# Softmax row sums taken by ones-products on TensorE, and casts, copies and normalising moved from VectorE to ScalarE

## The chip, the cores and the metric

The kernel runs on one core of one Trainium2 chip. The metric is the device time of one execution in microseconds (us); lower is better. Before the change it is 1401.03 us, the median of three runs (1400.17 to 1402.62).

## The reference, cut to what matters

Sixteen images of 256 x 256 go through an edge filter, 77 embedded text tokens are appended to each (333 rows of 256), and then come an attention layer over five windows of 128 rows and a mixture of eight experts:

```python
h = clip(sum(abs(conv2x2(x))), 0, 1)                 # (16, 256, 256)
h = concatenate([h, weight[x_txt]], axis=1)          # (16, 333, 256)
# attention, 16 heads of 16, windows of 128 rows with stride 64 (and the last 128 rows)
z = layernorm(h); q, k, v = z @ Wq + bq, z @ Wk + bk, z @ Wv + bv
scores = q_win @ k_win.T / sqrt(16) + pos_bias       # 128 x 128 for each head and window
out_win = softmax(scores) @ v_win
merged = scatter_add(out_win) / counts               # rows in two windows are averaged
h = h + merged @ Wo + bo
# experts: softmax gate, top 2 of 8, silu(x @ w1) * (x @ w3) @ w2, weighted and added
h = h + moe(layernorm(h))
```

## The kernel before, in words

All is written out by hand for five engines that run side by side and meet in semaphores. There are two stages. The first takes the images one after the other through the attention layer, the router and a scatter of the rows into regions by expert. The second takes 91 tiles of 128 rows through the expert products; the change does not touch its code.

**The first stage.** A loop `run_steps` calls `step(b, par)` for each image b on every engine, and inside it a loop over k = 0 to 19. One k, called a step here, stands for one group: a window (5 of them, `NW`) times four heads (`GH`), so 5 x 4 = 20 groups (`G`) for an image. The groups go through a pipeline, the same on every engine:

- TensorE at step k: scores of group k into `s_bank` (L1026, four bf16 products), transposes of the probabilities of group k-3 into `t_bank` (L1040, four), products with V of group k-4 into `o_bank` (L1063, four products of 32 columns of weights, one for each strip of 32 output rows; they show as eight records in the trace). On every fourth group of a window it also transposes a tile `weight` (L1072, two products).
- VectorE at step k: adds the bias to the scores of group k and takes the row minimum into `neg_max` (L757, a custom instruction and the reading of its accumulator, four of each).
- ScalarE at step k: exp of group k-1 with the row sum (L622, four ACTIVATEs, each followed by an ACTIVATION_READ_ACCUMULATOR), then the copy of the transposed probabilities of group k-2 to `probsT` (L636, three groups of four; the fourth is copied by VectorE in L772).

**The row sums before.** The row sums land as `row_sum` with the query rows on the partitions, while the outputs in `o_bank` have the head's columns on the partitions. So once for each window VectorE inverts 16 sums for each row (L768), spreads them over 256 columns as `weight` (L776), TensorE transposes that (L1072), ScalarE copies the transposed tile to `weightT` (L642), and VectorE multiplies it with the outputs into `head_out` (L784). GpSimd adds `head_out` to `ctxT` (L520).

**What else hangs on the steps.** Each step also carries work of neighbouring images at fixed k. On TensorE: transposes of the normalised rows `xn` (k = 0, L1082), the router's counting products (k = 2, L1089 and L1093), the Q and K projections (k = 2 to 5, L1104), the output projection (k = 6 and 7, L1004), the V projection (k = 10 and 11, L1011), transposes of the second layernorm's `rows` (k = 16, L1134), the gate product (k = 18, L1142). ScalarE moves `xT` (k = 0, L648), `qk` (k = 2 to 5, L660) and `x2T` (k = 16, L667) out of PSUM. VectorE does both layernorms' statistics and normalising (L714), the casts of `qk` into bf16 parts (L733, L738), V's bias (L745), absolute values of the filter (L851), and the router. GpSimd does the filter's differences, the splitting of `qk` into three bf16 parts (L502, L507), the inverse root, and the scatters.

**The stacks.** Q and K of an image enter the scores as bf16 parts stacked on 96 partitions. They go there by way of DRAM: SyncE's queue writes each part with two transfers (L366, `qk_parts`), and reads it back with six transfers for Q and six for K (L372, `stacks`). Before, it issues five of the six pairs of writes, then waits for all of Q's parts and reads them, then writes the last pair, stores the image's rows, waits for all of K's parts, and reads K. The scores of the next image wait for all twelve reads (`stack_in`).

## Time and profile before

| | |
|---|---|
| median of 3 runs | 1401.03 us |
| the profiled execution | 1394.69 us, its span 1392.9 us, the rest lies around the span |
| TensorE busy | 1189.1 us (85% of the span) |
| VectorE busy | 920.9 us (66%) |
| ScalarE busy | 782.9 us (56%) |
| GpSimd busy | 611.8 us (44%) |
| granted TensorE clock, mean | 0.919 |

The shares are averages over the two stages, which differ: read them apart. Times below are microseconds from the span's start. A start-to-start distance of two neighbouring rows of one engine says what an instruction takes of the engine's time; its own length is longer, since neighbours overlap.

### The profile page before, as it was taken

The page shows a single profiled execution, that of the slowest core. Times are in us where ns is not written, and L with a number is a line of the kernel's source. Part 1 is how long each engine was busy: PE and PEld are TensorE (multiplying, and loading weights), DVE is VectorE, ACT ScalarE, POOL GpSimd, SP SyncE. Part 2 cuts the span into 40 slices and gives each one's busy share as a digit, 9 for nine tenths or more (in the row PEclk, how much of TensorE's full clock was granted, in tenths as well). Part 3 has the DMA queues.
Part 4 walks back from the last instruction along what each step waited for, and adds up shares of the span by engine and source line. Part 5 has one row for each costly group of instructions (what it writes and reads, how often), then busy time and mean ns, then how long its engine had stood idle before and what let it go on. Part 6 is the DMA issues. An engine that isn't in the chain of part 4 may idle for free.

```text
span 1392.9 us, 35049 instructions
## 1 busy us (share of the span) xinstructions
PE 1189.1 (85%) x10190; PEld 951.8 (68%) x10191; DVE 920.9 (66%) x4211; ACT 782.9 (56%) x3176; POOL 611.8 (44%) x900
## 2 busy tenths in 40 slices
PE   2386888988988998888889872999999999999996
PEld 1254656655655665555556551999999999999995
DVE  4485989888888889898997864344444444444442
ACT  0196998989899998899899980211111111111110
POOL 5333466565646655665665334122322232232232
PEclk9698899889898988999998985899999999999998
DMA  3694563465357446634643507232233323323222
GB/s 110 133 234 100 109 132 89 95 131 113 88 103 142 92 92 116 128 89 94 133 107 71 96 24 234 36 50 46 49 47 48 49 45 49 48 46 48 46 49 31
DMA packets 98402, 123.36 MB, mean 89 GB/s; under 512 B 15544, under 2 KB 87416, under 8 KB 95192
## 3 DMA queue, kind: packets, MB, share of 16 engines
q1 hardware_dynamic: 75880, 89.96, 30.6%
q0 software_dynamic: 18576, 24.47, 10.9%
q10 hardware_dynamic: 3808, 7.34, 1.8%
q8 instruction: 57, 0.93, 0.3%
q14 instruction: 81, 0.66, 0.2%
HBM read 69.35 MB, written 46.07 MB: 83 GB/s over the span
## 4 chain that ended last, share of the span: by engine, by line
PE 47%; POOL 16%; issue 14%; DMA 12%; ACT 4%; SPq 3%; DVE 3%; POOLq 0%; DVEq 0%; ACTq 0%
PE s_bank L1168 12%; PE t_bank L1168 12%; PE o_bank L1183 11%; DMA qk_parts<-parts_flat 5%; POOL expert_slots L493 4%; DMA expert_slots<-rows,slot_i 4%; DMA stacks<-qk_parts 3%; PE m_bank L1104 3%; ACT probs L622 3%; PE t_bank L1040 2%; SPq L372 2%; POOL rest L502 2%; PE o_bank L1063 2%; POOL parts_flat L507 2%; PE m_bank L1157 1%
## 5 line engine op out<-in xcount | busy, mean ns | idle before, releaser
L622 ACT ACTIVATE probs<-probs,neg_max 128x128 f32<-128x128 f32 x1280 | 497.4, 401 | 21.6 <-DVE neg_max L757 21.0
L757 DVE CUSTOM_DVE_ANT_0 probs<-s_bank,nbias 128x128 f32<-128x128 f32 x1280 | 293.0, 284 | 38.4 <-PE s_bank L1026 36.9
L622 ACT ACTIVATION_READ_ACCUMULATOR probs<-probs,neg_max 128x1 f32 x1280 | 257.4, 201 | 0.0
L1040 PE MATMUL t_bank<-ident,probs 128*128 128x128 f32 x1280 | 221.0, 300 | 28.7 <-ACT probs L622 26.7
L681 ACT ACTIVATE v_all<-s_bank 128x512 f32<-128x512 f32 x91 | 54.4, 598 | 286.9 <-PE s_bank L1168 286.9
L1026 PE MATMUL s_bank<-stacks 96*128 96x128 bf16 x1280 | 136.5, 233 | 68.8 <-DMA stacks<-qk_parts 46.9
L1026 PEld LDWEIGHTS s_bank<-stacks 96*128 96x128 bf16 x1280 | 93.4, 105 | 132.4 <-DMA stacks<-qk_parts 50.7
L1040 PEld LDWEIGHTS t_bank<-ident,probs 128*128 128x128 f32 x1280 | 150.1, 153 | 45.7 <-ACT probs L622 41.7
L636 ACT ACTIVATE probsT<-t_bank 128x512 f32<-128x512 f32 x240 | 141.9, 591 | 57.5 <-PE t_bank L1040 56.7
L1183 PE MATMUL o_bank<-stacks,v_all 128*128 x728 | 172.6, 380 | 0.7 <-issue 0.5
L597 POOL DMA_INDIRECT out_dram<-wq_sb,nbias x46 | 75.7, 1645 | 198.5 <-DVE wq_sb L967 185.3
L1063 PE MATMUL o_bank<-probsT,v_all 128*32 128x128 f32 x2560 | 146.0, 303 | 16.9 <-ACT probsT L636 9.7
L597 POOL DMA_INDIRECT out_dram<-wk_sb,nbias x45 | 73.3, 1629 | 172.8 <-DVE wk_sb L967 170.0
L973 DVE TENSOR_TENSOR v_all<-v_all,t_bank 128x512 f32<-128x512 f32 x91 | 62.6, 688 | 127.1 <-PE t_bank L1168 127.1
L1183 PEld LDWEIGHTS o_bank<-stacks,v_all 128*128 128x128 f32 x728 | 131.3, 190 | 16.0 <-issue 1.8
L675 ACT ACTIVATE v_all<-m_bank 128x256 f32<-128x256 f32 x91 | 35.0, 384 | 143.3 <-PE m_bank L1157 143.3
L493 POOL DMA_INDIRECT expert_slots<-rows,slot_i x96 | 100.0, 1042 | 29.3 <-issue 21.7
L1063 PEld LDWEIGHTS o_bank<-probsT,v_all 128*32 128x32 f32 x2560 | 52.9, 112 | 79.0 <-issue 50.0
L757 DVE DVE_READ_ACCUMULATOR2_ANT neg_max<- 128x1 f32 x1280 | 103.8, 81 | 0.1
L1168 PEld LDWEIGHTS s_bank<-v_all,probs 128*128 128x128 f32 x736 | 91.0, 195 | 3.2 <-ACT v_all L675 0.9
L1168 PE MATMUL s_bank<-v_all,probs 128*128 128x128 f32 x736 | 91.4, 278 | 0.5 <-ACT v_all L675 0.5
L1168 PE MATMUL t_bank<-v_all,probs 128*128 128x128 f32 x736 | 90.7, 277 | 0.0
(158 smaller groups left out, 2079.4 us busy)
## 6 DMA issues: line engine op xcount, KB each, us to landing
stacks<-qk_parts SPq DMA_DIRECT2D x192, 166.5 KB, 5.6
qk_parts<-parts_flat SPq DMA_DIRECT2D x192, 83.2 KB
nbias<-expert_slots SPq DMA_DIRECT2D x91, 129.0 KB, 2.0
w_sb<-in_L_ffn_w_dram ACTq DMA_DIRECT2D x14, 512.0 KB, 5.2
v_all<-v_all SPq DMA_DIRECT2D x64, 96.0 KB, 6.4
x_here<-in_x_dram SPq DMA_DIRECT2D x16, 256.0 KB, 5.7
out_dram<-h_res SPq DMA_DIRECT2D x16, 256.0 KB
stacks<-in_L_ffn_w_dram SPq DMA_DIRECT2D x8, 512.0 KB, 8.5
```

The source lines that it names most:

```text
L493: pool.indirect_dma_start(slots_dram[:, :], bass.IndirectOffsetOnAxis(slot_i[0:n, kk, j:j + 1], 0), rows[0:n, kk, j, :], None).then_inc(sc ...
L597: pool.indirect_dma_start(out[:, :], bass.IndirectOffsetOnAxis(g_rows[r][:, D + 1:D + 2].bitcast(I32), 0), y_sb[r], None, compute_op=ALU.a ...
L622: ins = act.activation(seg, seg, ACT.Exp, bias=neg_max[:, r, i:i + 1], scale=-1.0, accum_out=row_sum[:, (par + v) % 2, h:h + 1])
L636: act.activation(probsT[:, k % 2, :], t_bank[:, k % 2, :], ACT.Copy).then_inc(pT_by_act, 1)
L681: act.activation(hidT[r % 2], s_bank[:, r % 2, :], ACT.Silu).then_inc(silu_ready, 1)
L757: ins = dve.tensor_tensor_reduce(probs[:, r, i * WIN:(i + 1) * WIN], s_bank[:, k % 2, i * WIN:(i + 1) * WIN], nbias[:, h, :], 1.0, BIG, AL ...
L973: dve.tensor_tensor(hidT[r % 2], hidT[r % 2], t_bank[:, r % 2, :], ALU.mult).then_inc(hid_ready, 1)
L1026: mm = pe.matmul(s_bank[:, k % 2, i * WIN:(i + 1) * WIN], q_stack[par][0:KROWS, h, lo:lo + WIN], k_stack[par][0:KROWS, h, lo:lo + WIN], st ...
L1040: mm = pe.transpose(t_bank[:, (k - 3) % 2, i * WIN:(i + 1) * WIN], probs[:, r, i * WIN:(i + 1) * WIN], ident[:, :])
L1063: mm = pe.matmul(o_bank[32 * i:32 * i + 32, vp, (g // 2) * WIN:(g // 2 + 1) * WIN], v_win[bp][:, w, c0:c0 + 2 * HD], probsT[:, (k - 4) % 2 ...
L1168: mm = pe.matmul(bank[:, par, n * P:(n + 1) * P], up_w[par][:, m, a, n * P:(n + 1) * P], gxT[par][:, a * P:(a + 1) * P], start=(a == 0), s ...
L1183: mm = pe.matmul(o_bank[:, r % 2, 0:D], hidT[r % 2][:, a * P:(a + 1) * P], w2_sb[:, bass.ds(e, 1), a, :].rearrange("p o n -> p (o n)"), st ...
```

## The change

- The row sums are no longer taken by exp. After the four products with V of a group, TensorE makes four more of the same form with a constant tile `head_of` of ones and zeros in the place of V. The sums then land in `o_bank` in the layout of the outputs, each repeated over the 16 columns of its head.
- VectorE inverts these, 128 columns at a time, twice a window, straight from PSUM into `weightT`, and multiplies. The tiles `row_sum`, `inv_sum`, `weight`, the transposes of `weight` and ScalarE's copy of them are gone.
- ScalarE copies all four groups of a window to `probsT`. It also takes over from VectorE: the high bf16 part (a second ACTIVATE out of PSUM beside that to `qk`), the middle part, the moving of V, the absolute values, and both normalisings, as ACTIVATEs with a scale and a bias for each row (the bias, minus mean times inverse root, is two instructions more on GpSimd).
- V's bias is folded into the output's bias once, with a product at the start.
- Several pieces stand at another k: ScalarE's moves of `xT` (0 to 1), `qk` (2-5 to 3-6), V (12, 13), `x2T` (16 to 17), the second normalising (VectorE's 14 to ScalarE's 15), the output projection (6, 7 to 7, 8), GpSimd's adding of a window (two steps later). The router's products go to `m_bank`.
- SyncE's queue reads each part back as soon as that part is written, with a semaphore for each part.

The core of the diff (names and constants, the first stage's other moves of k, and the counts of semaphores are left out):

```diff
 SyncE
-                    write_part(0, 0, part1_ready)
-                    write_part(1, 0, part1_ready)
-                    write_part(0, 1, part2_ready)
-                    write_part(0, 2, part3_ready)
-                    write_part(1, 1, part2_ready)
+                    write_part(0, 0, part1_ready, b1 * 4 + 2)
+                    write_part(1, 0, part1_ready, b1 * 4 + 4)
                     if b >= 1:
                         sp.wait_ge(scores_done, (b1 - 1) * G)
-                    load_stack(0, q_stack[par1], Q_SLOTS)
-                    write_part(1, 2, part3_ready)
+                    load_stack(0, 0, q_stack[par1], Q_SLOTS)
+                    write_part(0, 1, part2_ready, b1 * 2 + 1)
+                    load_stack(1, 0, k_stack[par1], K_SLOTS)
+                    write_part(0, 2, part3_ready, b1 * 2 + 1)
+                    load_stack(0, 1, q_stack[par1], Q_SLOTS)
+                    write_part(1, 1, part2_ready, b1 * 2 + 2)
+                    load_stack(0, 2, q_stack[par1], Q_SLOTS)
+                    write_part(1, 2, part3_ready, b1 * 2 + 2)
+                    load_stack(1, 1, k_stack[par1], K_SLOTS)
                     if tail:
                         store_h2()
-                    load_stack(1, k_stack[par1], K_SLOTS)
+                    load_stack(1, 2, k_stack[par1], K_SLOTS)
...
 ScalarE
+                def normalise(src, rstd, shift, dst, done):
+                    for j in range(NT):
+                        act.activation(dst(j), src[:, j, :], ACT.Identity, bias=shift[:, j:j + 1],
+                                       scale=rstd[:, j:j + 1]).then_inc(done, 1)
...
-                            ins = act.activation(seg, seg, ACT.Exp, bias=neg_max[:, r, i:i + 1], scale=-1.0,
-                                                 accum_out=row_sum[:, (par + v) % 2, h:h + 1])
+                            ins = act.activation(seg, seg, ACT.Exp, bias=neg_max[:, r, i:i + 1], scale=-1.0)
                         ins.then_inc(exp_ready, 1)
...
-                    if proj and k in (2, 3, 4, 5):
+                    if proj and k in (3, 4, 5, 6):
...
+                        for dst, done in ((qk[:, 2 * n + c, :], qk_ready), (parts[:, 2 * n + c, 0, :], part1_ready)):
+                            act.activation(dst, m_bank[:, c, 0:S], ACT.Identity,
+                                           bias=(bq_col if n == 0 else bk_col)[:, c:c + 1],
+                                           scale=(-SCALE if n == 0 else 1.0)).then_inc(done, 1)
+                    if proj and k == 7:
+                        part_middle(0)
+                    if proj and k == 9:
+                        part_middle(1)
...
+                    if tail and k == 15:
+                        act.wait_ge(rstd2_ready, b0 + 1)
...
+                        normalise(h_res[1 - par], rstd2, shift2, lambda j: rows[:, 0, j, 0:D], rows0_ready)
-                    if tail and k == 16:
+                    if tail and k == 17:
                         act.wait_ge(x2T_done, b0 + 1)
...
 VectorE
-                        dve.reciprocal(inv_sum[:, vp, :], row_sum[:, vp, :]).then_inc(inv_ready, 1)
-                        dve.tensor_copy(probsT[:, k % 2, :], t_bank[:, k % 2, :]).then_inc(pT_by_dve, 1)
-                        dve.tensor_copy(weight[:, vp, :, :], inv_sum[:, vp, :].unsqueeze(2).to_broadcast([P, H, HD]))\
-                            .then_inc(weight_ready, 1)
+                    v, c = ((k - 8) // NG, 0) if k % NG == 0 else ((k - 10) // NG, 1)
+                    if k % 2 == 0 and ((att and v >= 0) or (tail and v < 0)):
...
+                        dve.reciprocal(weightT[:, c * WIN:(c + 1) * WIN],
+                                       o_bank[:, vp, (C + c) * WIN:(C + c + 1) * WIN]).then_inc(inv_ready, 1)
+                        if c == 1:
...
+                            dve.tensor_tensor(head_out[:, vp, :], o_bank[:, vp, 0:C * WIN], weightT[:, :], ALU.mult)\
+                                .then_inc(head_ready, 1)
...
 TensorE
+                        for i in range(GH):
+                            mm = pe.matmul(o_bank[32 * i:32 * i + 32, vp, (C + g // 2) * WIN:(C + g // 2 + 1) * WIN],
+                                           head_of[:, (g % 2) * HD:(g % 2) * HD + 2 * HD],
+                                           probsT[:, (k - 4) % 2, i * WIN:(i + 1) * WIN],
+                                           start=False, stop=(g % 2 == 1), skip_group_check=True)
                         mm.then_inc(pv_done, 1)
-                        if g == 3:
-                            pe.wait_ge(weight_ready, b * NW + m // NG + 1)
-                            for c in range(C):
-                                mm = pe.transpose(o_bank[:, vp, (C + c) * WIN:(C + c + 1) * WIN], ...)
...
-                            pe.wait_ge(qk_ready, b1 * 4 + c + 1)
+                            pe.wait_ge(part1_ready, b1 * 4 + c + 1)
```

**TensorE, step k = 4.** Before, the K projection stands behind transposes and products whose results ScalarE moved at k = 2:

```order
L1026 MATMUL s_bank<-stacks 128x128 [waits max_ready]
L1026 MATMUL s_bank<-stacks 128x128 x3
L1040 MATMUL t_bank<-ident,probs 128x128 [waits pT_by_dve,exp_ready]
L1040 MATMUL t_bank<-ident,probs 128x128 x3
L1063 MATMUL o_bank<-probsT,v_all 32x128 [waits prefix_read,v_shift_in,head_ready,v_ready,pT_by_act]
L1063 MATMUL o_bank<-probsT,v_all 32x128 x3
L1104 MATMUL m_bank<-xT,wk_sb 128x333 [waits qk_ready]
L1104 MATMUL m_bank<-xT,wk_sb 128x333
```

Now, at the same place (the lines of the changed kernel are numbered anew; L1053 are the products with ones):

```order
L1018 MATMUL s_bank<-stacks 128x128 [waits max_ready]
L1018 MATMUL s_bank<-stacks 128x128 x3
L1029 MATMUL t_bank<-ident,probs 128x128 [waits pT_ready,exp_ready]
L1029 MATMUL t_bank<-ident,probs 128x128 x3
L1047 MATMUL o_bank<-probsT,v_all 32x128 [waits v_shift_in,head_ready,v_ready,pT_ready]
L1047 MATMUL o_bank<-probsT,v_all 32x128 x3
L1053 MATMUL o_bank<-probsT,head_of 32x128 x4
L1096 MATMUL m_bank<-xT,wk_sb 128x333 [waits part1_ready]
L1096 MATMUL m_bank<-xT,wk_sb 128x333
```

Four products came in, and the projection waits for the second of the two moves of ScalarE instead of the only one.

**ScalarE, steps k = 2 and 3.** Before, the first move of Q stands in k = 2, in front of the exp and the copy of k = 3:

```order
L622 ACTIVATE probs,row_sum<-probs,neg_max 128x128 [waits max_ready]
L622 ACTIVATE probs,row_sum<-probs,neg_max 128x128 x3
L636 ACTIVATE probsT<-t_bank 128x512 [waits pv_done,pT_done]
L660 ACTIVATE qk<-m_bank,bq_col 128x333 [waits rest_ready,qk_done]
L622 ACTIVATE probs,row_sum<-probs,neg_max 128x128 [waits max_ready]
L622 ACTIVATE probs,row_sum<-probs,neg_max 128x128 x3
L636 ACTIVATE probsT<-t_bank 128x512 [waits pv_done,pT_done]
```

Now k = 2 carries the absolute values (`diag`, `anti`), and the first move of Q, to `qk` and to `parts_flat`, stands behind the copy of k = 3:

```order
L655 ACTIVATE probs<-probs,neg_max 128x128 [waits max_ready]
L655 ACTIVATE probs<-probs,neg_max 128x128 x3
L667 ACTIVATE probsT<-t_bank 128x512 [waits pv_done,pT_done]
L677 ACTIVATE score_e<-below_best 128x24 [waits payload_ready,below_ready]
L681 ACTIVATE diag<-diag 128x512 [waits diffs_ready]
L681 ACTIVATE anti<-anti 128x512
L655 ACTIVATE probs<-probs,neg_max 128x128 [waits max_ready]
L655 ACTIVATE probs<-probs,neg_max 128x128 x3
L667 ACTIVATE probsT<-t_bank 128x512 [waits pv_done,pT_done]
L691 ACTIVATE qk<-m_bank,bq_col 128x333 [waits parts_out0_0,rest_ready,qk_done]
L691 ACTIVATE parts_flat<-m_bank,bq_col 128x333
```

The move went behind one more wait for TensorE's transposes (`pT_done`), and became two.

**SyncE's queue, the parts of one image.** Before, from the second pair of writes for Q on to the reading of K:

```order
L366 DMA qk_parts<-parts_flat 8x16x333 [waits part2_ready]
L366 DMA qk_parts<-parts_flat 8x16x333
L372 DMA stacks<-qk_parts 16x5328 [waits parts_out0,scores_done]
L372 DMA stacks<-qk_parts 16x5328 x5
L366 DMA qk_parts<-parts_flat 8x16x333 [waits part3_ready]
L366 DMA qk_parts<-parts_flat 8x16x333
L357 DMA out_dram<-h_res 128x2x256 [waits h2_ready]
L358 DMA out_dram<-h_res 77x256
L372 DMA stacks<-qk_parts 16x5328 [waits parts_out1]
L372 DMA stacks<-qk_parts 16x5328 x5
```

Now, in the middle of an image:

```order
L375 DMA stacks<-qk_parts 16x5328 [waits parts_out0_0,scores_done]
L375 DMA stacks<-qk_parts 16x5328 x2
L368 DMA qk_parts<-parts_flat 8x16x333 [waits part2_ready]
L368 DMA qk_parts<-parts_flat 8x16x333
L375 DMA stacks<-qk_parts 16x5328 [waits parts_out1_0]
L375 DMA stacks<-qk_parts 16x5328 x2
L368 DMA qk_parts<-parts_flat 8x16x333 [waits part3_ready]
L368 DMA qk_parts<-parts_flat 8x16x333
L375 DMA stacks<-qk_parts 16x5328 [waits parts_out0_1]
L375 DMA stacks<-qk_parts 16x5328
L368 DMA qk_parts<-parts_flat 8x16x333 [waits part2_ready]
L368 DMA qk_parts<-parts_flat 8x16x333
```

Reads that stood behind all writes of Q now stand between the writes, each with a wait for its own part.

## Rows read from the trace of the kernel before

**Rows 1.** Busy us by stretch: PE, PEld, DVE, ACT, POOL; clock, DMA share, GB/s.
```profile
0.00:63.00 63.00, 11.85 (x34) 7.83 (x35) 25.73 (x45) 4.17 (x6) 29.02 (x64) 0.86 0.53 113
63.00:829.00 766.00, 657.25 (x6274) 449.02 (x6274) 650.38 (x3717) 684.72 (x2975) 416.72 (x716) 0.90 0.52 110
```

**Rows 2.** Waits of TensorE from 60 to 860: total us, times, longest.
```profile
PE s_bank L1026 <- DMA stacks<-qk_parts: 46.9, 11, 23.3
PE t_bank L1040 <- ACT probs L622: 26.7, 50, 1.3
PE s_bank L1026 <- DVE neg_max L757: 21.3, 44, 1.4
PE o_bank L1072 <- DVE weight L776: 17.1, 14, 1.3
```

**Rows 3.** TensorE in order of time, one image: start, us, instruction, idle before.
```profile
449.23 0.61 PE L1026 MATMUL s_bank<-stacks 96*128 96x128 bf16 x4 [2.06 <-DMA stacks<-qk_parts]
...
458.09 0.43 PE L1063 MATMUL o_bank<-probsT,v_all 128*32 128x128 f32 x8
458.44 0.44 PE L1072 MATMUL o_bank<-ident,weight 128*128 128x128 f32 x2
458.72 1.29 PE L1104 MATMUL m_bank<-xT,wq_sb 128*128 128x333 f32 x4
459.84 0.39 PE L1026 MATMUL s_bank<-stacks 96*128 96x128 bf16 x4
...
470.86 0.40 PE L1026 MATMUL s_bank<-stacks 96*128 96x128 bf16 x4
...
472.00 0.40 PE L1026 MATMUL s_bank<-stacks 96*128 96x128 bf16 x4
...
495.98 0.60 PE L1026 MATMUL s_bank<-stacks 96*128 96x128 bf16 x4 [0.84 <-DMA stacks<-qk_parts]
```

**Rows 4.** SyncE's queue in order of time, that image.
```profile
475.77 2.76 SPq L372 DMA_DIRECT2D stacks<-qk_parts  x6
...
486.68 3.31 SPq L372 DMA_DIRECT2D stacks<-qk_parts  x6
```

**Rows 5.** ScalarE in order of time.
```profile
451.49 0.40 ACT L622 ACTIVATE probs<-probs,neg_max 128x128 f32<-128x128 f32 x1
451.78 0.20 ACT L622 ACTIVATION_READ_ACCUMULATOR probs<-probs,neg_max 128x1 f32 x1
451.87 0.40 ACT L622 ACTIVATE probs<-probs,neg_max 128x128 f32<-128x128 f32 x1
...
461.25 0.59 ACT L636 ACTIVATE probsT<-t_bank 128x512 f32<-128x512 f32 x1
461.72 0.38 ACT L642 ACTIVATE weightT<-o_bank 128x256 f32<-128x256 f32 x1
461.99 0.54 ACT L660 ACTIVATE qk<-m_bank,bq_col 128x333 f32<-128x333 f32 x1
462.41 0.41 ACT L622 ACTIVATE probs<-probs,neg_max 128x128 f32<-128x128 f32 x1
```

**Rows 6.** Groups by form from 60 to 860: busy us, mean ns, idle before.
```profile
L784 DVE TENSOR_TENSOR head_out<-o_bank,weightT 128x256 f32<-128x256 f32 x80 | 33.7, 421 | 19.2 <-ACT weightT L642 19.0
...
L520 POOL TENSOR_TENSOR ctxT<-ctxT,head_out 128x256 f32<-128x256 f32 x40 | 32.4, 810 | 119.1 <-DVE head_out L784 118.1
...
L768 DVE RECIPROCAL inv_sum<-row_sum 128x16 f32<-128x16 f32 x80 | 19.8, 248 | 3.3 <-ACT probs L622 3.2
...
L816 DVE RECIPROCAL score_inv<-score_sum 128x3 f32<-128x3 f32 x16 | 2.8, 176 | 0.6
```

**Rows 7.** The chain that ended last, from 0 to 100.
```profile
40.83 2.62 DMA qk_parts<-parts_flat
...
46.75 7.06 DMA qk_parts<-parts_flat
...
63.43 0.61 PE s_bank L1026 x4
```

More of the change, by code:

```diff
@@ L220, in build @@
         part3_ready = sem("part3_ready")
-        parts_out = [sem(f"parts_out{n}") for n in range(2)]
+        parts_out = [[sem(f"parts_out{n}_{t}") for t in range(3)] for n in range(2)]
         stack_in = sem("stack_in")
@@ L521, in step @@
                                            ALU.add).then_inc(ctx_added, 1)
+                for k in range(G):
+                    if tail and k == 12:
+                        if b0 >= 1:
+                            pool.wait_ge(rows0_ready, b0 * 3)
+                        pool.wait_ge(ln2_step, b0 * 6 + 6)
+                        inverse_root(moments2, neg_mean2, rstd2, shift2, root2_step, b0, rstd2_ready)
+                    add_window(k)
                     if inp and k == 0:
@@ L648, in step @@
                         act.activation(xT[:, :, :], m_bank[:, :, 0:S], ACT.Copy).then_inc(xT_ready, 1)
-                    if tail2 and k == 1:
+                    if tail2 and k == 2:
                         act.wait_ge(below_ready, b9 + 1)
@@ L723, in step @@
                     dve.tensor_scalar(bq_col[:, :], bq_col[:, :], -SCALE, None, ALU.mult).then_inc(prep_done, 1)
+                    for c in range(C):
+                        dve.tensor_copy(bv_wide[:, c, :], bv_col[:, c:c + 1].to_broadcast([P, P])).then_inc(bv_spread, 1)
+                    dve.wait_ge(bv_done, 1)
+                    dve.tensor_tensor(bo_row[:, :], bo_row[:, :], o_bank[:, 0, 0:D], ALU.add).then_inc(bo_ready, 1)
                 if b == 0:
@@ L787, in step @@
+                    if tail2 and k == 1:
                         if b9 >= 1:
@@ L852, in step @@
-                    if tail and k == 8:
+                    if tail2 and k == 5:
+                        dve.wait_ge(score_e_ready, b9 + 1)
+                        if b9 >= 1:
+                            dve.wait_ge(scattered, b9 * 96)
+                        dve.tensor_reduce(score_sum[:, :], score_e[:, :, :], AX.X, ALU.add).then_inc(payload_ready, 1)
+                        dve.tensor_copy(rows[:, :, :, D + 1].bitcast(I32),
+                                        token_f[:, :].unsqueeze(1).to_broadcast([P, K, NT])).then_inc(payload_ready, 1)
+                        dve.wait_ge(payload_ready, b9 * 4 + 2)
+                        dve.reciprocal(score_inv[:, :], score_sum[:, :]).then_inc(payload_ready, 1)
+                        dve.tensor_scalar(token_f[:, :], token_f[:, :], float(S), None, ALU.add).then_inc(token_step, 1)
+                        dve.wait_ge(payload_ready, b9 * 4 + 3)
+                        dve.tensor_tensor(rows[:, :, :, D].rearrange("p k j -> p j k"), score_e[:, :, 0:K],
+                                          score_inv[:, :].unsqueeze(2).to_broadcast([P, NT, K]), ALU.mult)\
+                            .then_inc(payload_ready, 1)
+                        dve.wait_ge(token_step, b9 + 1)
@@ L853, in step @@
+                    if tail and k == 9:
                         dve.wait_ge(wo_done, b0 * 2 + 2)
@@ L982, in _ @@
             for n in range(2):
-                dve.wait_ge(parts_out[n], PARTS_OUT * B)
+                for t in range(3):
+                    dve.wait_ge(parts_out[n][t], PART_OUT * B)
             dve.wait_ge(qk_done, 4 * B)
```

369 lines of the change are left out of this document (155 added, 214 removed).

## The prediction

> **What bounds the kernel now.** I read the busy time by stretch first, then TensorE's waits, then one image in order of time on TensorE, SyncE's queue and ScalarE, then the groups by form, and the chain of the start. The experts' stage is untouched, so all of the change lies before 852 us. From 63 to 829 us sixteen images pass in 766 us, 47.9 us each, at a mean granted clock of 0.90 [rows 1]. For an image TensorE is busy 657.25 / 16 = 41.1 us, ScalarE 42.8 and VectorE 40.6: three engines at 85 to 89%, none full. What sets the period is partly a loop outside them: the scores of an image wait for the reading of the stacks, 2.06 us in one image and 0.84 us in the next [rows 3], 46.9 us over 11 waits with 23.3 us of it at the start, so 23.6 us over 15 images or 1.5 us each [rows 2]. The queue shows why: K is read from 486.68 on, after the wait for its last part, and the next image's first scores begin at 495.98 [rows 3, 4]. TensorE's other waits in this stage are for exp (26.7), for the row minimum (21.3) and for the tile of inverses (17.1): 65.1 / 16 = 4.1 us an image [rows 2].
>
> A mean clock of 0.90 between 1.0 and 0.5 means a fifth of the time at 1.2 GHz. If a fifth of the 41.1 busy us (8.2) ran at half speed, it would have taken 4.1 at 2.4 GHz, so TensorE's work is 41.1 - 4.1 = 37.0 us an image at full clock. The period is then 37.0 work + 4.1 half clock + 6.8 waits (1.5 for the stacks, 4.1 for the three others, 1.2 of small ones).
>
> **TensorE's work.** The products with V of a group take from 458.09 to 458.44, 0.35 us, and the ones-products have the same form, moving tile and strips: 20 x 0.35 = 7.0 us more an image. The transposes of `weight` go, 458.44 to 458.72, 0.28 us: 5 x 0.28 = 1.4 less [rows 3]. Work becomes 37.0 + 5.6 = 42.6 us. A step without extra work goes from 1.14 us (470.86 to 472.00) to 1.49.
>
> **ScalarE.** An exp that sums is 0.38 us from start to start, and its accumulator's reading begins 0.29 us after it [rows 5]. Without the reading I take 0.29, so 80 x 0.09 = 7.2 us less; from below it can't be under the 0.27 that a 256-column move without a row operand takes (461.72 to 461.99), from above it stays 0.38. The moves of `weight` go: 5 x 0.27 = 1.35 less. Added: five copies of 512 columns at 0.47 (2.35); four more moves of 333 columns with a bias at 0.42 (1.7); two casts of 666 columns, on the line through 256 columns (0.38) and 512 (0.59) 0.72 long and 0.61 from start to start (1.2); three moves of V at 0.27 (0.8); two absolute values at 0.47 (0.95); six normalising ACTIVATEs. For these the line gives 0.27; a row operand adds 0.09 (333 columns would be 0.44 without it and are 0.54 [rows 5]), two make 0.45, 2.7 us in all. Sum +9.7 - 8.55 = +1.2 us: from 42.8 to 44 us. ScalarE isn't relieved, it swaps one load for another. A bare step of it becomes 4 x 0.29 + 0.47 = 1.65, from 2.0.
>
> **VectorE.** It loses, for a window, the copy of a group, the spreading and the 16-column inverse, and gains two inverses of 128 columns. The inverse is 176 ns for 3 columns and 248 for 16 [rows 6], 5.5 ns a column, so 248 + 112 x 5.5 = 0.87 us; the lower bound is a column's usual cost, some 0.3 us, the upper twice the estimate, 1.7. I take 0.87, as it extrapolates the same operation. That is about what goes, and the casts, normalisings, moves of V and absolute values leave as well, so VectorE falls by several us an image and stops limiting: the 38.4 us of waits for the minimum and the inverses (2.4 an image) go nearly all.
>
> The Trainium skill, VectorE: DVE Perf Modes, First, the fixed hardware budget, says that the reciprocal is an iterative divide with a repeat count of 8. Read as eight cycles an element it would make some 1.2 us of one inverse, an estimate from that page, and the forecast about 5 us higher; the two rows give a smaller slope.
>
> **The handovers are what I expect to cost most.** ScalarE at step k copies group k-2, and the transposes of that group stand in TensorE's step k+1. So whatever ScalarE does behind its copy in step k falls beside TensorE's step k+1. After those transposes TensorE has only 0.35 + 0.35 = 0.70 us of products before its extra work of k+1, while ScalarE needs 0.5 for the copy and then the move. Before, the consumer stood two steps behind; now the order shows it one step behind, in these places, for each image:
> - k = 2: the first Q product needs `xT`, moved in ScalarE's step 1: 0.5 + 0.7 - 0.7 = 0.5 us, 0.6 with the semaphores.
> - k = 4 and k = 5: the K products need both moves of the bank, in steps 3 and 4: 0.5 + 0.42 + 0.54 + 0.15 for semaphores - 0.7 = 0.9 us, say 1.0 each.
> - k = 7: the output projection needs the last window's `ctxT`. VectorE makes it in step 6 after its minimum: 0.2 for the scores + 0.9 for the row minimum (an estimate: it must fit in the bare step of 1.14 us) + 0.87 + 0.42, GpSimd adds in 0.81 [rows 6], 3.3 us with semaphores, and TensorE is there after 2 x 1.49 = 3.0: 0.4 us.
> - k = 16: the transposes of `rows` need the normalising of ScalarE's step 15: 0.5 + 3 x 0.45 + 0.25 - 0.7 = 1.4 us.
> - k = 18: the gate product needs `x2T` of step 17: 0.6 us.
>
> Sum 5.0 us an image. Queued behind each of these waits are the next group's scores and transposes, and behind them VectorE's minimum and ScalarE's next copy, so ScalarE, filled to 44 us, can't use most of the pause. Bare steps after k = 12, where ScalarE's 1.65 exceeds TensorE's 1.49 and moves of V and normalisings come on top, I give 1.0 us of waits for exp (1.7 before).
>
> **The stacks.** The queue now alternates writes and reads. A write lands 2.62 us after the issue ends when nothing is ahead of it, 7.06 when six reads are [rows 7]; K's six reads took 9.3 us to be usable [rows 3, 4]. With at most three reads ahead of a write I take 2.6 to 5.5 us. There are twelve reads at about 1.1 us of transfer (the 9.3 us less an idle landing of 2.62, by six) and twelve writes of half the bytes at about half, some 20 us. The last high part is ready after seven steps of 2.4 to 2.9 us, most with a projection, at about 18 us of the image; from there, with some pauses of the queue, they end at 41 to 43, against a period of 48. So the 1.5 us wait goes. At the start the wait of 23.3 us is on the end's path [rows 2]; there the reads that begin earlier save about 5 us. In the first image 14 transfers of expert weights share the engines, and the five waits in series cost more than two did: +2 us.
>
> **The clock.** The half-clock steps of the image shown follow the pause for the stacks: 449.23 to 495.98 holds both [rows 3]. With that pause gone and bare steps filled to 1.49 of 1.65 us, I take 1.0 us of the 4.1; bounds are 0 and 4.1, since the handovers are pauses too.
>
> **Sum.** 42.6 work + 5.0 handovers + 1.0 for exp + 0.2 small + 1.0 clock = 49.8 us against 47.9: +1.9 an image, 15 periods, +28 us. With -5 at the start and +2 in the first image it is +25. The profiled execution took 1394.7 us (span 1392.9 and 1.8 around it), which gives 1419.7; the median of the runs is 1401.0, 6.3 above it, so the forecast is 1425 us.
>
> **Rivals.**
> - *The removed pauses win (faster).* The stack wait, VectorE's waits and half clock go, and the handovers are half of mine, because ScalarE has already finished its exp and starts the copy as each transposed bank ends. For it: ScalarE is busy 42.8 of 47.9 us, so it stands ready for 5 us of each image. Against it: its copy can't start before the transposes end, however early it is. Then 42.6 + 2.5 + 1.0 + 0.2 + 0 = 46.3, -1.6 x 15 - 3 = -27: 1374 us.
> - *The queue sets the period (slower).* If each of the five waits in series costs the 7.06 us of rows 7 because reads are always ahead, then 18 + 5 x 7.06 less the issues that overlap gives 51 us before the next image's scores, +3.1 x 15 = +47, and no gain at the start: 1448 us. It decides from a landing of about 6.5 us on. Against it: only one write in twelve waited so long, behind six reads.
> - *Slow inverses.* At the upper bound of 1.7 us the handover at k = 7 grows by 0.8 us, +12: 1437 us. VectorE has room for the rest.
> - *The exp without its sum is not faster.* At 0.38 ScalarE has 44 + 7.2 = 51.2 us of work and about 2 of waits: 53, +77 us, 1478. Against it: the reading is a row of its own with 0.20 us.
>
> Chances: forecast 0.54, faster rival 0.24, queue 0.10, inverses 0.09, exp 0.03. A change within 0.2% is about what a measurement of this kernel can't tell from none; forecast and faster rival spread by some 15 us each, so I put 0.05 there, 0.23 faster and 0.72 slower. The forecast's own range, with the clock from 0 to 4.1 and handovers from 4 to 6, is 1400 to 1450; down to 1372 takes in half of the faster rival, and 1452 the queue.
>
> **What would show it.** Right: after the change TensorE waits for ScalarE's `part1`, `rows` and `rest` moves, about 1 us or more each and once or twice an image; the wait for `stacks` is gone but for the start, which is under 20 us; exp is 0.29 from start to start; ones-products fill 0.35 us; the period is 49 to 51 us. Wrong: a period under 47.5 with handover waits under 3 us an image, a wait for `stacks` at each image, or a clock still at 0.90.

## The result, and the profile after

The changed kernel takes 1477.51 us (median of 4 runs, 1476.24 to 1479.21) against 1401.21 (1400.17 to 1402.62) before: ratio 1.0545, interval 1.0526 to 1.0563, slower. The forecast was 1425 us, with 1452 as the upper end of its range: the sign was right, the size was not.

| | before | after |
|---|---|---|
| profiled execution, its span | 1394.69, 1392.9 | 1477.90, 1476.1 |
| first scores | 63.43 | 57.30 |
| period of an image (start of the transposes of `xn` to the next, mean of the thirteen between the third and the last) | 47.9 | 53.3 |
| experts' stage, from its first product | 521.7 | 521.3 |

The loss is all in the first stage. The two profiled executions differ by 83.2 us: 6 come back at the start, 7 go in the first image, 13 x 5.46 = 71 in the thirteen periods, and 12 in the last images up to the experts. (The medians differ by 76, as the profiled execution before lay 6.3 us under its median.) The busy time over exactly these thirteen periods, in the columns of [rows 1], after and then before:

```profile
119.03:812.27 693.24, 573.73 (x7124) 413.38 (x7120) 474.47 (x2819) 582.27 (x1606) 360.03 (x683) 0.94 0.43 96
```

```profile
118.19:740.42 622.23, 544.65 (x5175) 372.98 (x5171) 548.12 (x3071) 562.50 (x2435) 365.02 (x631) 0.91 0.52 106
```

TensorE is busy 573.73 / 13 = 44.1 us of an image after, and waits the other 9.2. The same 7124 records take 41.6 us an image in a version below whose clock is 1.00 over its thirteen periods, so that is the work at full clock, and 2.5 us are half clock. Before, TensorE is busy 41.9 us and waits 6.0; a clock of 0.91 means 18% of the time at 1.2 GHz, so of the 41.9 an estimated 3.8 are half clock and 38.1 work. The waits of TensorE after, over the same thirteen periods, in the columns of [rows 2]:

```profile
PE m_bank L1126 <- ACT rows L645: 30.8, 13, 2.4
PE m_bank L1096 <- ACT parts_flat L691: 25.6, 26, 1.2
PE m_bank L1079 <- ACT xT L672: 17.8, 12, 1.6
PE t_bank L1029 <- ACT probs L655: 13.4, 26, 0.7
PE m_bank L1133 <- ACT rest L715: 8.2, 13, 1.0
PE m_bank L996 <- POOL ctxT L535: 5.8, 7, 0.9
PE m_bank L996 <- POOL w_sb L535: 5.2, 6, 1.0
PE m_bank L1096 <- DVE region_end L836: 3.5, 10, 0.4
```

Of [rows 2] the wait for the stacks is left at two places, 34.8 us in all: at the start (19.2 us) and in the first image; those for the minimum and for `weight` are gone, and in their place stand waits for results that a move or an addition makes one step ahead of their product (`parts_flat` stands for the K products, `rest` for the gate product, which reads the tile named x2T in the code). The second wait for the stacks, after and then before:

```profile
116.62 0.61 PE L1018 MATMUL s_bank<-stacks 96*128 96x128 bf16 x4 [15.58 <-DMA stacks<-qk_parts]
```

```profile
116.21 0.61 PE L1026 MATMUL s_bank<-stacks 96*128 96x128 bf16 x4 [12.46 <-DMA stacks<-qk_parts]
```

So [rows 2] held this one too, and the 1.5 us an image that the forecast read there were (46.9 - 23.3 - 12.5) / 15 = 0.7. One image of TensorE in order of time, which answers to [rows 3]:

```profile
494.53 0.43 PE L1047 MATMUL o_bank<-probsT,v_all 128*32 128x128 f32 x8
494.77 0.40 PE L1053 MATMUL o_bank<-probsT,head_of 128*32 128x128 f32 x8
495.10 0.40 PE L1018 MATMUL s_bank<-stacks 96*128 96x128 bf16 x4
...
497.71 0.17 PE L1079 MATMUL m_bank<-taken,before 128*128 128x24 bf16 x1 [1.19 <-ACT xT L672]
...
504.39 1.39 PE L1096 MATMUL m_bank<-xT,wk_sb 128*128 128x333 f32 x4 [0.97 <-ACT parts_flat L691]
...
508.00 1.39 PE L1096 MATMUL m_bank<-xT,wk_sb 128*128 128x333 f32 x4 [0.97 <-ACT parts_flat L691]
...
532.31 0.40 PE L1053 MATMUL o_bank<-probsT,head_of 128*32 128x128 f32 x8
535.08 1.37 PE L1126 MATMUL m_bank<-ident,rows 128*128 128x128 f32 x6 [2.37 <-ACT rows L645]
536.24 0.63 PE L1018 MATMUL s_bank<-stacks 96*128 96x128 bf16 x4
536.67 1.06 PE L1029 MATMUL t_bank<-ident,probs 128*128 128x128 f32 x4
```

The products with V now take 0.24 us (494.53 to 494.77) and the ones-products 0.33 (to 495.10), together 0.22 more than the 0.35 of before: of two sets in a row the first takes the shorter time. And after the pause of 2.37 us in front of `rows` the same scores take 0.63 us for 0.40 and the transposes 1.06 for 0.60: half clock. The granted clock is 1.00 from 530.0 to 532.5 us, before the pause, and 0.50 from 535.0 to 540.0. ScalarE beside the K products and beside `rows`, which answers to [rows 5]:

```profile
506.49 0.60 ACT L667 ACTIVATE probsT<-t_bank 128x512 f32<-128x512 f32 x1 [1.00 <-PE t_bank L1029]
506.98 0.53 ACT L691 ACTIVATE qk<-m_bank,bq_col 128x333 f32<-128x333 f32 x1
507.40 0.54 ACT L691 ACTIVATE parts_flat<-m_bank,bq_col 128x333 bf16<-128x333 f32 x1
507.82 1.27 ACT L655 ACTIVATE probs<-probs,neg_max 128x128 f32<-128x128 f32 x4
...
531.79 1.28 ACT L655 ACTIVATE probs<-probs,neg_max 128x128 f32<-128x128 f32 x4
532.96 0.60 ACT L667 ACTIVATE probsT<-t_bank 128x512 f32<-128x512 f32 x1
533.43 1.59 ACT L645 ACTIVATE rows<-h_res,shift,rstd 128x256 f32<-128x256 f32 x3
```

At the K products ScalarE stands idle 1.00 us for transposes, then copies and moves while TensorE stands idle 0.97: the two take turns. Beside `rows` it is the other way: the transposes that it copies at 532.96 ended at 532.1 (begun at 531.48, 0.66 long), but ScalarE was still at exp. It starts some 0.8 us late, and TensorE waits for that too. The inverse by form, for [rows 6]:

```profile
L799 DVE RECIPROCAL weightT<-o_bank 128x128 f32<-128x128 f32 x160 | 152.5, 953 | 0.1
```

### The profile page after: what moved, and what is told of

Read it like the earlier page. It is cut to its first block, busy times and chain, and to the rows that moved or that the text cites. A ratio compares the mean times of both kernels' runs of the same rounds, so it can differ in the third digit from the quotient of the medians.

```text
span 1476.1 us, 38491 instructions
## 1 busy us (share of the span) xinstructions
PE 1229.4 (83%) x12594; PEld 1004.6 (68%) x12595; DVE 829.3 (56%) x3894; ACT 811.8 (55%) x2168; POOL 608.2 (41%) x967
## 4 chain that ended last, share of the span: by engine, by line
PE 58%; ACT 16%; issue 16%; DMA 4%; POOL 3%; DVE 2%; SPq 1%; POOLq 0%; ACTq 0%; DVEq 0%
PE s_bank L1159 11%; PE t_bank L1159 11%; PE o_bank L1174 11%; ACT probs L655 6%; PE t_bank L1029 6%; ACT probsT L667 4%; PE m_bank L996 3%; DMA qk_parts<-parts_flat 3%; PE m_bank L1003 3%; PE s_bank L1018 3%; PE o_bank L1047 2%; PE m_bank L1096 2%; ACT rows L645 2%; PE m_bank L1133 2%; PE o_bank L1053 1%
## 5 line engine op out<-in xcount | busy, mean ns | idle before, releaser
L655 ACT ACTIVATE probs<-probs,neg_max 128x128 f32<-128x128 f32 x1280 | 407.8, 400 | 11.8 <-DVE neg_max L788 11.8
L667 ACT ACTIVATE probsT<-t_bank 128x512 f32<-128x512 f32 x320 | 190.0, 594 | 148.6 <-PE t_bank L1029 145.5
L1029 PE MATMUL t_bank<-ident,probs 128*128 128x128 f32 x1280 | 214.3, 294 | 18.7 <-ACT probs L655 16.8
L1018 PE MATMUL s_bank<-stacks 96*128 96x128 bf16 x1280 | 136.8, 232 | 39.4 <-DMA stacks<-qk_parts 34.8
L799 DVE RECIPROCAL weightT<-o_bank 128x128 f32<-128x128 f32 x160 | 152.5, 953 | 0.1
L1053 PE MATMUL o_bank<-probsT,head_of 128*32 128x128 f32 x2560 | 136.9, 286 | 1.2 <-issue 1.2
L505 POOL DMA_INDIRECT expert_slots<-rows,slot_i x96 | 100.0, 1042 | 32.4 <-issue 23.3
L515 POOL TENSOR_TENSOR rest<-qk,parts_flat 128x666 f32<-128x666 f32 x32 | 45.0, 1407 | 145.0 <-ACT qk L691 135.8
L1047 PEld LDWEIGHTS o_bank<-probsT,v_all 128*32 128x32 f32 x2560 | 51.7, 111 | 61.1 <-issue 46.9
## 6 DMA issues: line engine op xcount, KB each, us to landing
qk_parts<-parts_flat SPq DMA_DIRECT2D x192, 83.2 KB
```

The source lines that it names most:

```text
L505: pool.indirect_dma_start(slots_dram[:, :], bass.IndirectOffsetOnAxis(slot_i[0:n, kk, j:j + 1], 0), rows[0:n, kk, j, :], None).then_inc(sc ...
L655: ins = act.activation(seg, seg, ACT.Exp, bias=neg_max[:, r, i:i + 1], scale=-1.0)
L667: act.activation(probsT[:, k % 2, :], t_bank[:, k % 2, :], ACT.Copy).then_inc(pT_ready, 1)
L799: dve.reciprocal(weightT[:, c * WIN:(c + 1) * WIN], o_bank[:, vp, (C + c) * WIN:(C + c + 1) * WIN]).then_inc(inv_ready, 1)
L1018: mm = pe.matmul(s_bank[:, k % 2, i * WIN:(i + 1) * WIN], q_stack[par][0:KROWS, h, lo:lo + WIN], k_stack[par][0:KROWS, h, lo:lo + WIN], st ...
L1029: mm = pe.transpose(t_bank[:, (k - 3) % 2, i * WIN:(i + 1) * WIN], probs[:, r, i * WIN:(i + 1) * WIN], ident[:, :])
```

## The experiments

Each run has its own comparison with the kernel before (1395.9 to 1399.2 us on these chips), so gains are taken as differences of two ratios, times 1400 us; with the intervals of the ratios such a gain is known to some 5 to 10 us. Periods, busy times and waits of one image are means over the thirteen periods named above; a gain for each image is the gain in time by 15.

### One handover undone at a time

`h_qk`, the Q and K moves:

```diff
-                    if proj and k in (3, 4, 5, 6):
-                        n, c = (k - 3) // 2, (k - 3) % 2
+                    if proj and k in (2, 3, 4, 5):
+                        n, c = (k - 2) // 2, (k - 2) % 2
```

> The changed kernel with one edit: ScalarE's moves of Q and K (to qk and to the high part) stand at k = 2 to 5 again. Theory of the handovers: TensorE's wait of its K products for ScalarE's moves, 29.6 us in the changed kernel, falls under 5 us, and the time falls by 25 to 35 us, to about 1447 us. Rival, TensorE's ones-products set the period: nothing falls, 1470 to 1480. Rival, the longer chain from the inverses to the output projection: nothing falls.

Measured 1436.19 us, ratio 1.0265 (1.0224 to 1.0305): 39 us less than the changed kernel, 4 more than the upper end of what was expected.

`h_rows`, the second normalising at 14 and the move of `x2T` at 16:

```diff
-                    if tail and k == 15:
+                    if tail and k == 14:
...
-                    if tail and k == 17:
+                    if tail and k == 16:
```

> The changed kernel with two moves taken back on ScalarE: the second normalising at k = 14 instead of 15, x2T at k = 16 instead of 17. Handovers: the waits for rows (44.3 us) and for x2T (10.1) fall under 12 us together and the time falls by 30 to 45 us, to about 1437. Rival, TensorE's work: no change beyond 10 us, since the pauses would only move.

Measured 1427.21 us, 1.0201 (1.0140 to 1.0261): 48 less, a little over the expected range too. `h_xt`, the move of `xT` at k = 0 for 1:

> The changed kernel with one thing undone: ScalarE's move of xT at k = 0 again. It removes a wait of 19.4 us in all (13 times). Together with the 41 us of Q and K alone and the 50 us of rows and x2T alone it makes up the 116 us of all, if the places add up: 25 us less than the changed kernel, 1450 to 1456. If the places only pass the wait on to each other until all are gone: 1465 to 1476.

Measured 1441.46 us, 1.0324 (1.0273 to 1.0375): 31 less, more than expected. `h_all`, all three at once, the version called repaired below:

> The changed kernel with all four of ScalarE's handovers one step earlier (xT 0, Q and K 2 to 5, second normalising 14, x2T 16). Handovers: their waits, 103 us together, fall under 30, half clock falls with them, and the time falls by 65 to 90 us, to 1390 to 1412. Rival, TensorE's added work of 3 us an image: 1455 or more, as only a part of 80 us can be got back. Rival, the new order of the queue: the wait for the stacks comes up instead, over 2 us an image.

Measured 1361.20 us (1359.81 to 1362.86), 0.9726 (0.9697 to 0.9756): 115 less than the changed kernel, and 38 less than the kernel before. The three parts sum to 118, so within the noise they add. All four expectations had the direction right and the size too small, for `h_all` by 25 us (65 to 90 less was expected). This is the version that beats both. Its thirteen periods, and all of TensorE's waits in them:

```profile
113.53:707.96 594.43, 540.70 (x7124) 389.51 (x7121) 485.81 (x2819) 570.27 (x1606) 359.65 (x683) 1.00 0.49 112
```

```profile
PE t_bank L1029 <- ACT probs L655: 10.0, 26, 0.4
PE m_bank L1126 <- ACT rows L645: 9.9, 13, 1.2
PE m_bank L1070 <- ACT xn L645: 8.7, 12, 0.7
PE m_bank L1096 <- DVE region_end L836: 8.2, 12, 0.7
PE m_bank L996 <- POOL ctxT L535: 5.2, 7, 0.8
PE m_bank L996 <- POOL w_sb L535: 4.9, 6, 1.0
```

The period is 594.43 / 13 = 45.7 us, busy 41.6 of it at a clock of 1.00, with the same 7124 records as the changed kernel, and 4.1 of waits. Of the 7.6 us between the two periods 5.1 are waits and 2.5 are clock. The waits for `xT`, K and `rest` are gone, that for `rows` is 0.8 us an image for 2.4.

### The handovers alone, in the kernel before

`b_late` is the kernel before with its moves of `xT`, Q, K and `x2T`, its splitting of Q and K and its second normalising one step later, and nothing else of the change (the output projection and the moves of V stay where they were, and VectorE still does the splitting's casts and the normalising). Two of the places:

```diff
-                    if proj and k in (2, 3, 4, 5):
-                        n, c = (k - 2) // 2, k % 2
+                    if proj and k in (3, 4, 5, 6):
+                        n, c = (k - 3) // 2, (k - 3) % 2
...
-                    if tail and k == 14:
+                    if tail and k == 15:
```

> The kernel before with nothing of the change but its later steps: the move of xT at k = 1 for 0, of Q and K at 3 to 6 for 2 to 5, the splitting and the second normalising (still VectorE's) one step later, the move of x2T at 17 for 16. Products, exp sums, inverses and queue stay as before. Handover theory (a product that stands one step behind its move makes TensorE wait, and it then runs at half clock): the K products wait about 1 us each, xT, rows and x2T 0.5 to 1.5 each, 3 to 4.5 us an image with the clock, and the stacks come up to one step later on top: 1445 to 1475 us. Rival, the ones-products and ScalarE's added load make the loss and the steps alone do not: 1400 to 1415.

Measured 1459.34 us, 1.0447 (1.0409 to 1.0485): +63 us with no ones-product, exp or queue touched.

```profile
PE s_bank L1026 <- DMA stacks<-qk_parts: 47.8, 12, 24.0
PE m_bank L1134 <- DVE rows L714: 33.4, 15, 10.3
PE t_bank L1040 <- ACT probs L622: 33.3, 52, 1.0
PE m_bank L1104 <- ACT qk L660: 26.9, 30, 1.0
PE m_bank L1104 <- ACT xT L648: 16.1, 15, 1.5
PE o_bank L1142 <- ACT rest L667: 15.9, 16, 1.6
```

The waits for `rows`, K (`qk` here), `xT` and `rest` are those of after; the kernel before has the K wait nowhere and each of the others only once, at an end of the stage. The parts of Q and K also reach the queue a step later, but that is not it: over the thirteen periods the wait for the stacks is 9.9 us in all, for 9.4 before. An image takes 52.0 us for 47.9, 3.0 more of it waits and 1.1 more busy time for the same 5175 records, at a clock of 0.88 for 0.91. With `h_all`, which keeps the products and ScalarE's load and is faster than the kernel before, this rules out the rival that these make the loss.

### ScalarE's lag

`l_dve` leaves every handover late, but gives the second normalising back to VectorE, still at k = 15 (the code of the kernel before).

> The changed kernel with one thing undone: the normalising of the rows by VectorE, but still at k = 15, all other handovers late. Lag theory: the rows' handover costs 2.8 us an image because ScalarE comes to k = 15 late from its absolute values and moves of V and then has three more instructions; on VectorE it falls to 1.2 to 1.7 us (1.65 in the kernel before with late handovers), with the clock some 2 us an image: 1440 to 1455 us. Rival, the distance of a step alone makes it, whoever does the work: 1465 to 1480.

Measured 1420.84 us, 1.0177 (1.0147 to 1.0206), 52 us less, better than either theory. Its thirteen periods, and its wait for `rows` in them:

```profile
116.27:764.54 648.27, 554.05 (x7124) 402.29 (x7121) 490.05 (x2858) 560.58 (x1569) 360.61 (x683) 0.96 0.46 103
```

```profile
PE m_bank L1132 <- DVE rows L761: 11.1, 13, 1.4
```

The rows' wait falls from 2.4 to 0.9 us an image. The period falls from 53.3 to 49.9 us: busy time from 44.1 to 42.6 for the same 7124 records, so 1.5 us are clock, and waits from 9.2 to 7.2, of which 1.5 are this row. What isn't settled is how much of the row's gain is ScalarE's lag, and how much its 1.7 us less of work an image.

### More products on TensorE

`ones2` makes the ones-products of the changed kernel twice, with constants of 0.5.

```diff
-            pool.memset(head_of[:, 0:HD], 1.0).then_inc(const_set, 1)
+            pool.memset(head_of[:, 0:HD], 0.5).then_inc(const_set, 1)
...
-                        for i in range(GH):
+                        for i in list(range(GH)) * 2:
```

> The changed kernel with the ones-products issued twice for each group, with 0.5 in the place of 1 so that the sums are the same. 20 x 0.33 = 6.6 us more of TensorE an image, 99 us over 15 periods if all is on the path. Handovers: in the steps where TensorE waits for ScalarE right behind them (k = 2, 4, 5, 7, 16, 18) they are hidden, so +55 to +80 us, and the waits there shrink. Rival, TensorE alone sets the period: +95 us or more.

Measured 1465.14 us, 1.0472 (1.0432 to 1.0511): 10 us faster than with half the products, where +55 to +80, or +95 and more, were expected. `h_ones2` is the same edit on the repaired kernel:

> The repaired kernel (handovers at their old distance, 1361 us) with the ones-products issued twice, their constants 0.5 for 1, so the sums are the same: 20 x 0.33 = 6.6 us more of products an image. If TensorE's work now sets the period and the clock is already high (0.98 in the first stage): +6.6 x 15, less the waits they cover (about 2 us an image): 1420 to 1460 us. Rival, the products buy back clock and waits as they did in the changed kernel, where they made it 12 us faster: under 1375.

Measured 1389.02 us, 0.9929 (0.9902 to 0.9955), +28.

```profile
314.19 0.62 PE L1053 MATMUL o_bank<-probsT,head_of 128*32 128x128 f32 x16
314.74 1.39 PE L1096 MATMUL m_bank<-xT,wk_sb 128*128 128x333 f32 x4
```

The doubled group takes 0.55 us for 0.33, so by these rows a set of ones-products costs 0.22 x 20 = 4.4 us an image, not the 7.0 of the forecast (nor the 6.6 of these expectations); the busy time of thirteen periods, 593.09 us for 540.70 at a clock of 1.00 in both, gives 4.0. Over 15 images that is 60 to 66 us, of which the repaired kernel pays 28. The changed one pays less than nothing: in `ones2` its busy time grows by only 2.4 us an image, since 1.6 of half clock go, its waits fall by 3.1, and its clock over the whole execution rises from 0.933 to 0.954. The numeric expectations of both runs missed on the high side.

### The other terms, priced on the repaired kernel

`h_expsum`, exp sums again into a tile that nobody reads (`accum_out=row_sum[...]`):

> The repaired kernel with exp summing again into a tile that nobody reads: 80 x 0.09 = 7.2 us more of ScalarE an image, from 43.6 to 50.8 of a period of 45.8. If exp's reading is what the removal of the sums saves: the period goes to 51 to 53, 1435 to 1470 us. If ScalarE had room: 1365 to 1390.

Measured 1452.98 us, 1.0383 (1.0345 to 1.0421), +92 us.

```profile
399.72 0.48 ACT L656 ACTIVATE probs<-probs,neg_max 128x128 f32<-128x128 f32 x1
400.01 0.28 ACT L656 ACTIVATION_READ_ACCUMULATOR probs<-probs,neg_max 128x1 f32 x1
400.10 0.48 ACT L656 ACTIVATE probs<-probs,neg_max 128x128 f32<-128x128 f32 x1
```

0.38 us from start to start with the reading, against 1.17 / 4 = 0.29 without: the term of the forecast stands, and is worth 6.1 of its 7.2 us an image.

`h_recip2`, each inverse of 128 columns made twice:

> The repaired kernel with each inverse of 128 columns made twice, the second into a spare tile: 10 x 0.95 us more of VectorE an image, from 35 to 45 of 45.8. At full cost on the chain to ctxT and in front of the minimum: 1390 to 1420 us. If VectorE has room for it: 1361 to 1372.

Measured 1418.52 us, 1.0160 (1.0122 to 1.0198): +61 us, 4.0 an image for 9.5 of VectorE. Its waits for `ctxT` and `w_sb` grow from 16.4 to 33.4 us, that for `region_end` from 8.6 to 19.4, that for the router's `taken` from 2.2 to 15.4, and one for `head_out` is new with 16.4; all of them are for VectorE's results or for GpSimd's sums of them. `h_oldsp`, SyncE's old order:

> The repaired kernel with SyncE's old order (all writes of Q and five of six in all first, Q read once, K read last behind the image's rows). The period is 45.8 us here, 2 shorter than before, so K's late reading should cost more than the 1.5 us an image of the kernel before: 3 to 4 us, and 5 at the start, 1405 to 1430 us. Rival, the order is worth only what it was in the kernel before (7 us): 1366 to 1372.

Measured 1433.28 us, 1.0242 (1.0170 to 1.0314): +72 us, a little over the expected range, and the wait for the stacks is back.

```profile
PE s_bank L1020 <- DMA stacks<-qk_parts: 51.3, 13, 23.3
PE m_bank L1128 <- ACT rows L647: 47.6, 16, 9.9
```

The stacks are the smaller part of it. Of the 4.9 us an image over the thirteen periods 2.0 are clock (43.6 us busy for 41.6 with the same work) and 2.9 are waits: 1.8 more for `rows`, 1.1 more for `taken`, 0.8 more for the stacks, less 0.8 at other places. In front of its normalising of `rows` ScalarE itself now stands idle 1.7 us an image, 0.03 in the repaired kernel, released by nothing that the profile shows.

`b_newsp`, the new order in the kernel before:

> The kernel before with nothing of the change but SyncE's order: each part read back as soon as it is written, a semaphore for each part. Theory (the wait for the stacks is 1.5 us an image and some 5 us of the start, and this order takes it away): 1375 to 1385 us. Rival, the waits in series of this order make a period of their own (the rival on the queue of the forecast): 1410 or more; a third, the stack wait only moves to the waits for exp and the minimum: 1393 to 1400.

Measured 1389.95 us, 0.9939 (0.9918 to 0.9960): 9 us less. The wait for the stacks falls from 46.9 to 34.7 us, 20.5 of it at the start and 14.2 in the first image, and the start gains 4 us (transposes of the second image at 59.70 for 63.83), but most periods stay at 47.9: the 0.7 us an image turns into other waits. None of the three ranges has the 9 us; the third is nearest. The same edit is worth 9 us here and 72 in the repaired kernel.

### Trying for more

`best1`, both normalisings on VectorE (k = 14 and 18) in the repaired kernel:

> The changed kernel with all handovers at their old distance and both normalisings given back to VectorE (at 14 and 18), which has 35 of 47 us of work an image; ScalarE loses 2.7 us of 44. If ScalarE's place behind the copies is what is left of the waits for rows (22.6 us in all with the normalising at 14 on ScalarE) and xn (9.4): 1335 to 1350 us. Rival, VectorE's six instructions stand in front of its minimum and delay the exp as much: 1358 to 1368.

`best2`, only the second one:

> The repaired kernel with one thing of the version with both normalisings on VectorE (1379.5 us): that of the rows at k = 14 on VectorE, that of xn left on ScalarE at k = 18. In the version with both, TensorE waited 25 us for VectorE in front of the transposes of xn and 4.4 for rows. If the loss was all xn's: 1345 to 1358 us. If the rows' three instructions in front of VectorE's minimum delay exp by what ScalarE saves: 1360 to 1368.

`h_head`, the inverses of a window in neighbouring steps, with the product and GpSimd's adding behind them:

> The changed kernel with all handovers at their old distance (moves of xT at k = 0, of Q and K at 2 to 5, normalising of the rows at 14, x2T at 16), and on top both inverses of a window taken in neighbouring steps, one step earlier for the second, the product with the outputs and GpSimd's adding with them. If the chain from the last ones-products to ctxT still costs the output projection 0.8 us an image, it goes here: 1361 less 10, 1345 to 1355 us. If the wait is only passed on to rows and probs: 1357 to 1364. If two inverses in two neighbouring steps make VectorE late with the minimum: 1370.

Measured: 1379.50 (0.9876, 0.9821 to 0.9931), 1365.33 (0.9757, 0.9717 to 0.9796) and 1411.55 us (1.0105, 1.0049 to 1.0162). None beats the repaired kernel, `best2` can't be told from it, and `best1` and `h_head` are slower than any range that was expected of them. In `h_head` TensorE waits for the router's `taken` from VectorE; that the second inverse now stands in front of it is read from the edit, not tested alone:

```profile
PE m_bank L1079 <- DVE taken L826: 32.5, 15, 2.3
```

## Why the prediction was wrong

**Failed: the sum of the handovers, 5.0 us an image, and the clock, 1.0.** The places and the direction were right, all five are in the trace. By place, predicted and measured (totals of the thirteen periods by 13): `xT` 0.6 and 1.4, K 2.0 and 2.0, `ctxT` 0.4 and 0.8 (the repaired kernel has 0.8 of it too), `rows` 1.4 and 2.4, `x2T` 0.6 and 0.6; `region_end` 0.3 was not foreseen. Sum 7.5. Where ScalarE is idle before the copy, at K, the price was exact. At `rows`, and by 0.4 us at `xT`, ScalarE was behind: I let its copy start when the transposes end, though I had myself put a bare step of it at 1.65 us against TensorE's 1.49. TensorE's measured 1.35 (494.53 to 495.88, from one set of products with V to the next) and ScalarE's 1.64 (494.73 to 496.37, from one copy to the next), so ScalarE falls behind by 0.3 us a bare step for the 0.16 of the forecast, and the two handovers behind such steps, `rows` and `xT`, pay the backlog too. At `rows` the three moves of V after ScalarE's last idle time (527.70 and 529.88) put 0.8 us more on it; I had named them, but only as a part of the waits for exp.

**The clock.** I let the half clock fall from 4.1 to 1.0 us because the pause for the stacks goes, and named the handovers only as a bound. It measured 2.5, and is gone when the handovers are repaired (clock 1.00 over the thirteen periods); in the kernel before, late handovers take the mean clock from 0.919 to 0.908. So the pauses that I added cost clock as the removed one had.

**Too high: the ones-products.** The work is 41.6 us for 42.6, as a set costs 0.20 to 0.22 and not 0.35 us. The increment was further off than that, 3.5 us for 5.6, but I had started it 1.1 too low: the 766 us of [rows 1] hold not sixteen images but 15.8 (6274 products, where a whole image has 5175 / 13 = 398), so TensorE was busy 41.9 us an image before and not 41.1. The two misses partly cancel, by luck. Together: 49.8 - 1.0 work + 1.5 clock + 3.0 waits (9.2 for 6.2) = 53.3. The profiled execution was 58 us over its forecast of 1419.7: sixteen images at 3.5, and one period of 1.9 more than the fifteen that I counted. The miss in the median is 52, since I added 6.3 us for a profiled execution below its median and the one after isn't.

**Right.** The exp without its sum (0.29); ScalarE, up 1.5 us an image (562.50 / 13 = 43.3 to 582.27 / 13 = 44.8) for the 1.2 of the forecast; TensorE's waits for exp, 1.0 us; the stacks: no image after the first waits for them, the start's wait is 19.2 us (under 20 was forecast), the queue issues the last read 41 us into an image, about as computed, and the start gained 6 for 5. The rival on the queue fell with that. Of [rows 7] the chain of the start after shows

```profile
41.14 7.10 DMA qk_parts<-parts_flat
49.22 4.72 DMA qk_parts<-parts_flat
...
57.30 0.62 PE s_bank L1018 x4
```

so a write did take over 7 us there, with three reads issued ahead of it, where I gave 2.6 to 5.5; so it doesn't take the six reads to which I put down the 7.06. It didn't set the period: in the thirteen periods the queue never waited over 3.2 us for a write. The inverse is 0.953 us, between my 0.87 from the slope of two rows and the 1.2 that the forecast estimated from the Trainium skill, VectorE: DVE Perf Modes, First, the fixed hardware budget. The page gives the repeat count of 8 and no time an element; reading it as eight cycles an element was mine, and it is too high in this case. But the rival on slow inverses priced 0.8 us more at only 12 us, while doubling each costs 61 in the repaired kernel: I counted only the handover at k = 7, and the runs show `region_end` and `head_out` waiting as well.

**The faster rival** gave 46.3 us, near the 45.7 of the repaired kernel, but that is luck: it kept 2.5 us of these handovers and 42.6 of work, where the repaired kernel has 41.6 of work and other waits. It failed here because it halved the handovers for a ready ScalarE. At `rows` and `xT` ScalarE isn't ready, and at K, where it is, the handover costs its full 1.0 us each all the same.

**Misread, without effect on the sum:** the stacks' wait of 1.5 us an image was 0.7 in a steady image and 12.5 once. The sum of the forecast was built from the terms of the changed kernel and did not use it.

**Open.** How the gain at `rows` in `l_dve` divides between ScalarE's backlog and its load; and what holds ScalarE in front of `rows` under the old queue order, which is the largest part of the waits that the repaired kernel gets back there.

## What to carry to other kernels

Moving a consumer's input from two steps behind to one cost more here than the sum of the instructions between: it also cost the producer's backlog at that point (1.0 us at `rows`) and the clock that the pauses lost (2.5 us an image). Compare the steps of the two engines in front of a handover first, with all that each carries there; the slower one arrives late at it. And price an edit in the schedule that it will run in: a queue order worth 9 us in one was worth 72 in the other.

## What was not expected of the hardware

More work on TensorE made the kernel faster: 4.0 to 4.4 us more products an image in the changed kernel, 10 us less in all, with the granted clock up from 0.933 to 0.954. And eight records of 32-column products behind eight of the same form cost 0.22 to 0.24 us, where the first set costs 0.33 to 0.35 with the turn to the next kind.
